# Depthwise convolution on TensorE: products in row order, copied out in token order

## The chip, the cores and the metric

One core of one Trainium2 chip. The metric is the device time of one execution in microseconds (us), median of three runs. Engines are named as the profile names them: PE is TensorE's matmul side and PEld its weight loads, DVE is VectorE, ACT is ScalarE, POOL is GpSimd, SP is SyncE.

## The reference, cut to what matters

The input is x, 4 images of 64 x 64 pixels with 256 channels, float32. Two layers follow each other. Layer 0, per pixel and per 2 x 2 window:

```
x_norm = layernorm(x);  x_proj, z = split(x_norm @ in_proj_W)          # 384 + 384 channels
y_ssm  = 0.5 * (scan over the 4 tokens of each 2x2 window, forward and backward)
y_dw   = depthwise 3x3 convolution of x_proj, padding SAME              # 9 taps, one weight per channel
y_conv = gelu(y_dw @ pw_W)
y      = (alpha * y_ssm + (1 - alpha) * y_conv) * silu(z) @ out_W
x_out  = x + y;  x = x_out + gelu(layernorm(x_out) @ fuse_W1 + b1) @ fuse_W2 + b2
```

Layer 1 is attention over the 4096 pixels of each image and a residual sum. The change touches only y_dw of layer 0.

## The kernel before, in words

Layer 0 walks over 32 tiles of 512 pixels (`TOK`), a tile being 8 rows of 64 pixels (`ROWS`). Within a tile the pixels are held in token order: the four positions (dr, dc) of a 2 x 2 window are four blocks of 128 pixels, inside a block by window row `wr` (4) and window column `wc` (32). Only `xp` (L217) is held in row order, with a border of one pixel: 10 rows of 66 floats for each of 3 channel blocks (`cb`). `inx` (L566, L569) fills it, and the convolution, the skip term (L595) and POOL's product (L689) read it.

The order of work is written out by hand in 48 ticks per tile: `OWN` lists the steps of tile k, `NEXT` the front steps of tile k+1, and `BACK` the closing steps of tile k-1. `body` (L529) gives PE, in each tick, three transposes of decay factors first (`turn_decays`, L510, one "fill" of a bank of `psD`), then the steps of the tick. DVE does the scan from these fills (`states`, L812: operations p, s, y), and its part of the other steps one tick later. The three `psD` banks let PE be three fills ahead: a fill waits for the DVE operation p (L865 or L868) that read the same bank three fills ago (L517 to L523).

The convolution of one channel block is three steps, a, b and c (rows dy = 0, 1, 2 of taps): ticks 8, 10, 11 for cb 0, ticks 13, 15, 17 for cb 1, ticks 19, 20, 21 for cb 2. A tap is a product with a diagonal matrix, `conv_w[:, cb, 3 * dy + dx, :]` (128 x 128, the tap's weights on the diagonal), accumulated over the nine taps in one bank of `psF`. Each tap has two products of 256 columns (L416 to L423), one for each row parity dr; its source takes every second row and, for each dc, every second pixel of `xp` (a step of two floats), so that the sums lie in PSUM in token order. After step c ACT copies the bank to `conv_sb` (the same memory as `y_ch`) in one instruction of 512 elements (L580). The pointwise product `pw` (L430, ticks 27 to 30) reads it.

`psF` has three banks, used in turn by the front jobs (`front_bank`, L121); PE waits for `front_out`, the count of ACT's copies, before it reuses one (L381). ACT's jobs are in the same order as PE's. Around the convolution stand the steps `ut` (PE transposes at L442, ACT copies at L608), `out` (PE at L470, after DVE's `y_ch` at L802), and in ticks 21 to 24 `xnt0`, `xnt1`, `xnth` (ACT L554, L557, DVE L758), `h2t` (ACT L622) and `w10` (PE L481, after L622). In tick 26 `proj` (PE L407) waits for DVE's L758.

The lines of PE's and ACT's part that the diff touches, with what calls them:

Of the kernel before, what the change touches and what calls it, by code (L numbers as in the profile page):

```python
# [14 lines left out]
ACT = mybir.ActivationFunctionType  # L15
# [5 lines left out]
B, H, W, C = 4, 64, 64, 256  # L21
# [10 lines left out]
ROWS = TOK // W  # L32
# [62 lines left out]
def exact(k):  # L95
    return isinstance(k, int)
# [67 lines left out]
def layer0(nc, keep, x, w, f_d, g_d, v_d, xres_d):  # L164
# [3 lines left out]
    with ctx:  # L168
# [18 lines left out]
        conv_w = sb("conv_w", [P, CB, 9, P])  # L187
# [29 lines left out]
        xp = sb("xp", [P, CB, ROWS + 2, W + 2])  # L217
# [19 lines left out]
        conv_sb = y_ch  # L237
# [129 lines left out]
        def _(pe):  # L367
# [3 lines left out]
            def front(step, f, par):  # L371
                if step.startswith(NOT_PSUM):
                    return
                kind, i = (step, "") if step in ("proj", "bct", "xnth") else (step[:-1], step[-1])
                job = step
                if step.startswith("conv"):
                    kind, i = "conv", step[4]
                    job = "conv" + i
                bank = psF[front_bank(f, job)]
                n, user = bank_user_before(f, job)  # L380
                if n is not None and not (kind == "conv" and step[-1] != "a"):  # L381
                    pe.wait_ge(front_out, n)
                    if user.startswith("xnt"):
                        pe.wait_ge(split_ok, SPLIT_JOBS * (iteration_of(f, job) + 2))
                if kind == "xnt":
                    if i == "0":
                        pe.wait_ge(stats1_ok, 5 * f + 5)
                    for t in range(T):
                        mm = turn(bank[:, t * P:(t + 1) * P], xf[:, t, int(i) * P:int(i) * P + P])
                elif kind == "xnth":  # L390
                    for kb in range(KB):
                        mm = turn(bank[:, kb * P:(kb + 1) * P], xf[:, T, kb * P:(kb + 1) * P])
                elif kind in ("inx", "z", "proj"):
                    if kind == "inx":
                        cb, dr = int(i) // 2, int(i) % 2
                        outs, src = bank[:, 0:TOK // 2 + W], [x[:, :, dr, :] for x in xnt]
                        wts = [x[:, :, cb * P:(cb + 1) * P] for x in in_w]
                    else:
                        outs = bank[:, :].rearrange("p (h n) -> p h n", h=2)
                        src = [x[:, :, :, 0:TOK // 2] for x in xnt]  # L400
                        c0 = INNER + int(i or 0) * P
                        wts = xproj_w if kind == "proj" else [x[:, :, c0:c0 + P] for x in in_w]
                    if kind == "proj":
                        pe.wait_ge(split_ok, SPLIT_JOBS * (f + 1))
                    for n, (a, b) in enumerate(((0, 0), (0, 1), (1, 0))):
                        for kb in range(KB):
                            mm = pe.matmul(outs, wts[a][:, kb, :], src[b][:, kb],  # L407
                                           start=n == 0 and kb == 0, stop=n == 2 and kb == KB - 1)
                elif kind == "bct":
                    pe.wait_ge(front_out, front_job(f, "proj"))  # L410
                    for t in range(T):
                        mm = turn(bank[:, t * P:(t + 1) * P], proj_sb[:, t * P:(t + 1) * P])
                elif kind == "conv":
                    cb, dy = int(i), "abc".index(step[-1])
                    for dx in range(3):
                        for dr in range(2):  # L416
                            src = xp[:, cb, dy + dr:dy + dr + ROWS - 1:2, dx:dx + W].rearrange(
                                "p wr (wc dc) -> p dc wr wc", dc=2)
                            mm = pe.matmul(bank[:, dr * 256:(dr + 1) * 256].rearrange(  # L419
                                "p (dc wr wc) -> p dc wr wc", dc=2, wr=ROWS // 2),  # L420
                                conv_w[:, cb, 3 * dy + dx, :], src,
                                start=dy == 0 and dx == 0, stop=dy == 2 and dx == 2,
                                skip_group_check=True)  # L423
                    if dy < 2:
                        return
                elif kind == "pw":
                    if i == "0":
                        pe.wait_ge(front_out, front_job(f, "conv2"))
                    for cb in range(CB):
                        mm = pe.matmul(bank[:, :], pw_w[:, cb, int(i) * P:int(i) * P + P], conv_sb[:, cb, :],  # L430
                                       start=cb == 0, stop=cb == CB - 1)
                elif step.startswith("dt"):
                    d, cb = "fb".index(step[2]), int(step[3])
                    r0 = 64 * d
                    mm = pe.matmul(bank[:, :], dt_w[r0:r0 + RANK, cb * P:(cb + 1) * P],
                                   proj_sb[r0:r0 + RANK, :], start=True, stop=True)
                elif step.startswith("ut"):
                    d, t = "fb".index(step[2]), int(step[3])
                    if t == 0:
                        pe.wait_ge(u_mul, 6 * f + 3 * (d + 1))  # L440
                    for cb in range(CB):
                        mm = turn(bank[:, cb * P:(cb + 1) * P], ut[:, cb, t * P:(t + 1) * P])  # L442
                mm.then_inc(front_full, 1)
# [98 lines left out]
        def _(act):  # L542
            def front(step, f, par):
# [28 lines left out]
                elif job == "proj":  # L572
                    last = nc.scalar.activation(proj_sb[:, :], bank[:, :], ACT.Identity, bias=proj_bias[:, :])
                elif job == "bct":
                    if not (exact(f) and f < 2):
                        act.wait_ge(state_ok, TILE_OPS * (f - 1))
                    src = bank[:, :].rearrange("p (t d r) -> p t d r", t=T, d=2)[:, :, :, RANK:RANK + 2 * STATES]
                    last = nc.scalar.activation(bc[:, par, :, :, :], src, ACT.Copy)
                elif job.startswith("conv"):
                    last = nc.scalar.activation(conv_sb[:, int(job[-1]), :], bank[:, :], ACT.Copy)  # L580
                elif job.startswith("dt"):
                    d, cb = "fb".index(job[2]), int(job[3])
                    if not (exact(f) and f == 0):
                        act.wait_ge(u_mul, 6 * (f - 1) + 3 * (d + 1))
                    last = nc.scalar.activation(dt[:, d, cb, :], bank[:, :], ACT.Silu,  # L585
                                                bias=col[:, dtb_c[d][cb]:dtb_c[d][cb] + 1])
                elif job.startswith("z"):
                    cb = int(job[-1])
                    if not (exact(f) and f == 0):
                        act.wait_ge(back_dve, emptied(f - 1, f"yt{cb}")[1])  # L590
                    for dr in range(2):
                        src = xp[:, cb, 1 + dr:dr + ROWS:2, 1:W + 1].rearrange("p wr (wc dc) -> p dc wr wc", dc=2)
                        dst = r_sb[:, cb, dr * 256:(dr + 1) * 256].rearrange(
                            "p (dc wr wc) -> p dc wr wc", dc=2, wr=ROWS // 2)
                        skip = nc.scalar.activation(dst, src, ACT.Copy, scale=mix[:, 2, cb:cb + 1])  # L595
                    skip.then_inc(skip_ok, 1)
                    last = nc.scalar.activation(q_sb[:, cb, :], bank[:, :], ACT.Silu,
                                                bias=in_bias[:, CB + cb:CB + cb + 1])
                elif job.startswith("pw"):
                    cb = int(job[-1])  # L600
                    if not (exact(f) and f == 0 and cb < 2):
                        act.wait_ge(r_ok, CB * f + cb - 1)
                    last = nc.scalar.activation(gel[:, cb % 2, :], bank[:, :], ACT.Gelu)
                elif job.startswith("ut"):
                    d, t = "fb".index(job[2]), int(job[3])
                    if t == 0 and not (exact(f) and f == 0):
                        act.wait_ge(state_ok, TILE_OPS * (f - 1) + DIR_OPS * (d + 1))
                    last = nc.scalar.activation(u[:, d, t, :], bank[:, 0:INNER], ACT.Copy)  # L608
# [845 lines left out]
```

## Time and profile before

| | |
|---|---|
| median of three runs | 5837.58 us |
| lowest and highest run | 5837.41 and 5845.89 us |
| span of the profiled execution | 5842.9 us, 100627 instructions |
| convolution products (L419) | 3456 records on PE, 397 ns each as listed |
| convolution copies (L580) | 96 on ACT |
| layer 0 | about the first 3560 us of the span |

No time of its own is given for the profiled execution; its span, first to last instruction, is 5.3 us (0.09%) over the median of the runs. A matmul with float32 operands shows as two records of PE and two weight loads: the 54 products of a tile (3 blocks x 9 taps x 2 parities) are 108 records, 12 in each of the nine steps. A record's listed length holds the time that it takes to pass through the array, so records overlap; what one costs PE is the distance from its start to the start of the next. A timeline merges like instructions that follow each other, with their number behind the x.

### The profile page before, as it was taken

How to read it: one execution, taken by the hardware profiler on the slowest of the kernel's cores; microseconds unless marked ns; L12 is line 12 of the kernel's file. 1: busy time of each engine (PE TensorE's matmuls, PEld its weight loads, DVE VectorE, ACT ScalarE, POOL GpSimd, SP SyncE). 2: the span in 40 equal slices, each digit the busy share in tenths (PEclk: the TensorE clock that was granted, in tenths of full speed). 3: DMA queues.
4: the chain of work that ended last, by engine and by line, in shares of the span. 5: the costliest groups of instructions: out<-in, count | busy, mean ns of one | idle time of the engine just before them, and what ended most of it. 6: DMA issues, size and time to landing. Idle time of an engine off the chain costs nothing. (4 is left out here: it accounts for less than half of the span.)

```text
span 5842.9 us, 100627 instructions
## 1 busy us (share of the span) xinstructions
PE 5433.9 (93%) x30696; PEld 4376.2 (75%) x30696; DVE 4398.7 (75%) x8598; ACT 3394.4 (58%) x5910; POOL 584.8 (10%) x658
## 2 busy tenths in 40 slices
PE   5999999999999999999999998899999999999998
PEld 4666666667667666666666665699889989988998
DVE  4888888887888788788878886676666667766666
ACT  3666666666666666666666664355555555555554
POOL 0111111111111110111111110100000000000000
PEclk8999999999999999999999999899999999999999
DMA  1010010010010010010000000300300030012000
GB/s 41 13 36 28 26 37 25 28 37 23 30 37 23 27 40 23 27 34 30 27 29 34 27 24 33 108 19 19 96 29 19 19 98 19 24 46 73 19 19 18
DMA packets 140892, 198.71 MB, mean 34 GB/s; under 512 B 19760, under 2 KB 107920, under 8 KB 140272
## 3 DMA queue, kind: packets, MB, share of 16 engines
q1 hardware_dynamic: 140272, 190.95, 10.3%
q8 instruction: 327, 5.36, 0.4%
q14 instruction: 293, 2.40, 0.1%
HBM read 111.22 MB, written 79.69 MB: 33 GB/s over the span
## 5 line engine op out<-in xcount | busy, mean ns | idle before, releaser
L1335 ACT ACTIVATE probs<-ps_s 128x512 f32<-128x512 f32 x1024 | 612.3, 598 | 1037.6 <-PE ps_s L1288 1037.6
L1346 DVE TENSOR_REDUCE part_max<-ps_m 128x1 f32<-128x512 f32 x1056 | 717.2, 691 | 576.1 <-PE ps_m L1268 575.9
L1297 PE MATMUL ps_o<-vh,ph 128*128 128x258 f32 x4096 | 1045.7, 288 | 31.6 <-ACT ph L1337 31.6
L1298 PE MATMUL ps_o<-vl,ph 128*128 128x256 f32 x4096 | 1037.1, 285 | 0.0
L369 PEld LDWEIGHTS psD<-ident,dec 128*128 128x128 f32 x4608 | 572.5, 144 | 491.0 <-DVE p_st L868 142.3
L369 PE MATMUL psD<-ident,dec 128*128 128x128 f32 x4608 | 784.2, 284 | 160.0 <-ACT dec L653 79.3
L868 DVE TENSOR_TENSOR p_st<-s_st,psD 128x384 f32<-128x384 f32 x1024 | 561.8, 549 | 490.0 <-PE psD L369 486.0
L419 PE MATMUL psF<-xp,conv_w 128*128 128x256 f32 x3456 | 862.4, 398 | 10.7 <-ACT u L608 10.3
L1297 PEld LDWEIGHTS ps_o<-vh,ph 128*128 128x128 f32 x4096 | 789.4, 193 | 48.1 <-issue 23.5
L653 ACT ACTIVATE dec<-dt,decay 128x384 f32<-128x384 f32 x1536 | 804.6, 603 | 2.3
L1298 PEld LDWEIGHTS ps_o<-vl,ph 128*128 128x128 f32 x4096 | 789.5, 193 | 0.0
L1370 DVE TENSOR_TENSOR pl<-probs,ph 128x512 fp32r<-128x512 f32 x1024 | 711.4, 695 | 69.6 <-ACT ph L1337 55.3
L419 PEld LDWEIGHTS psF<-xp,conv_w 128*128 128x128 f32 x3456 | 631.7, 189 | 155.8 <-ACT u L608 18.0
L1303 PEld LDWEIGHTS ps_o<-vh,pl 128*128 128x128 f32 x4096 | 627.9, 192 | 107.9 <-DVE pl L1370 34.7
L1303 PE MATMUL ps_o<-vh,pl 128*128 128x258 f32 x4096 | 681.3, 289 | 0.3
L871 DVE SCALAR_TENSOR_TENSOR s_st<-u,bc,p_st 128x384 f32<-128x384 f32 x1024 | 659.0, 651 | 0.0
L881 DVE SCALAR_TENSOR_TENSOR y_tok<-s_st,bc,y_tok 128x384 f32<-128x384 f32 x960 | 618.9, 645 | 0.0
L1337 ACT ACTIVATE ph<-ps_s 128x512 fp32r<-128x512 f32 x1024 | 608.5, 594 | 0.0
L689 POOL TENSOR_TENSOR ut<-dt,xp 128x256 f32<-128x256 f32 x384 | 341.6, 923 | 1886.8 <-ACT dt L585 1886.7
L1268 PE MATMUL ps_m<-f_max,gq 96*128 96x512 f32 x1056 | 416.7, 418 | 32.8 <-DMA gq<-queries_d 29.9
L1288 PE MATMUL ps_s<-gq,f_st 128*128 128x512 f32 x1024 | 409.6, 405 | 39.2 <-issue 37.4
L865 DVE SCALAR_TENSOR_TENSOR p_st<-u,bc,psD 128x384 f32<-128x384 f32 x512 | 303.2, 607 | 171.9 <-PE psD L369 100.9
(145 smaller groups left out, 7055.8 us busy)
## 6 DMA issues: line engine op xcount, KB each, us to landing
values_d<-v_st SPq DMA_DIRECT2D x64, 512.0 KB, 4.8
xf<-in_x_dram SPq DMA_DIRECT2D x128, 128.0 KB
xb<-in_x_dram SPq DMA_DIRECT2D x128, 128.0 KB
residual_d<-xb SPq DMA_DIRECT2D x32, 512.0 KB, 2.6
vh<-values_d SPq DMA_DIRECT2D x32, 512.0 KB, 5.0
vl<-values_d SPq DMA_DIRECT2D x32, 512.0 KB, 6.0
res<-residual_d SPq DMA_DIRECT2D x32, 512.0 KB, 3.3
out_dram<-res SPq DMA_DIRECT2D x128, 128.0 KB
```

The source lines that it names most:

```text
L369: return pe.transpose(out, in_, ident[:, :])
L419: mm = pe.matmul(bank[:, dr * 256:(dr + 1) * 256].rearrange("p (dc wr wc) -> p dc wr wc", dc=2, wr=ROWS // 2), conv_w[:, cb, 3 * dy + dx, ...
L653: nc.scalar.activation(dec[:, pair8 % 2, n, cb, :, :], dt[:, d, cb, first * P:(first + 3) * P].rearrange("p (t w) -> p t w", t=3), ACT.Exp ...
L871: nc.vector.scalar_tensor_tensor(s_t, u[:, d, token_of(d, step), :], scalar(step, n, "b"), p_t, ALU.mult, ALU.add).then_inc(state_ok, 1)
L881: nc.vector.scalar_tensor_tensor(y_t, src, scalar(step, n, "c"), y_t, ALU.mult, ALU.add).then_inc(state_ok, 1)
L1297: pe.matmul(ps_o[qt][:, 0:C + 2], lhs, vh[:, m, :], start=m == 0, stop=False, skip_group_check=True)
L1298: pe.matmul(ps_o[qt][:, 0:C], lhs, vl[:, m, :], start=False, stop=False, skip_group_check=True)
L1303: mm = pe.matmul(ps_o[qt][:, 0:C + 2], pl[:, m % 3, qt * P:(qt + 1) * P], vh[:, m, :], start=False, stop=m == KEYS - 1, skip_group_check=True)
L1335: nc.scalar.activation(probs[:, m % 3, :], ps_s[m % 2][:, :], ACT.Exp).then_inc(exp_ok, 1)
L1337: nc.scalar.activation(ph[:, m % 3, :], ps_s[m % 2][:, :], ACT.Exp).then_inc(exp_ok, 1)
L1346: nc.vector.tensor_reduce(part_max[:, qt, kc:kc + 1], ps_m[r % 2][:, :], AX.X, ALU.max).then_inc(max_out, 1)
L1370: nc.vector.tensor_tensor(pl[:, m % 3, :], probs[:, m % 3, :], ph[:, m % 3, :].bitcast(F32), ALU.subtract).then_inc(pl_ok, 1)
```

## The change

Each tap becomes one product of 512 columns whose source is 8 rows of 64 pixels of `xp`, in row order, and whose output is the whole bank in row order. ACT's copy becomes two ACTIVATEs of 256 elements, one for each dr, which read the bank with a step of two floats and write `conv_sb` in token order. The waits, the semaphore counts and the tick table stay.

```diff
                     for dx in range(3):
-                        for dr in range(2):
-                            src = xp[:, cb, dy + dr:dy + dr + ROWS - 1:2, dx:dx + W].rearrange(
-                                "p wr (wc dc) -> p dc wr wc", dc=2)
-                            mm = pe.matmul(bank[:, dr * 256:(dr + 1) * 256].rearrange(
-                                "p (dc wr wc) -> p dc wr wc", dc=2, wr=ROWS // 2),
-                                conv_w[:, cb, 3 * dy + dx, :], src,
-                                start=dy == 0 and dx == 0, stop=dy == 2 and dx == 2,
-                                skip_group_check=True)
+                        mm = pe.matmul(bank[:, :].rearrange("p (r w) -> p r w", r=ROWS), conv_w[:, cb, 3 * dy + dx, :],
+                                       xp[:, cb, dy:dy + ROWS, dx:dx + W],
+                                       start=dy == 0 and dx == 0, stop=dy == 2 and dx == 2)
...
                 elif job.startswith("conv"):
-                    last = nc.scalar.activation(conv_sb[:, int(job[-1]), :], bank[:, :], ACT.Copy)
+                    for dr in range(2):
+                        src = bank[:, :].rearrange("p (wr dr wc dc) -> p dr dc wr wc", dr=2, dc=2, wr=ROWS // 2)
+                        last = nc.scalar.activation(
+                            conv_sb[:, int(job[-1]), dr * 256:(dr + 1) * 256].rearrange(
+                                "p (dc wr wc) -> p dc wr wc", dc=2, wr=ROWS // 2), src[:, dr], ACT.Copy)
```

## Rows read from the trace of the kernel before

**Rows 1.** The page: busy time, share of the span, instructions; clock in 40 slices.

```profile
PE 5433.9 (93%) x30696; PEld 4376.2 (75%) x30696; DVE 4398.7 (75%) x8598; ACT 3394.4 (58%) x5910; POOL 584.8 (10%) x658
...
PEclk8999999999999999999999999899999999999999
```

**Rows 2.** Windows: length; PE, PEld, DVE, ACT, POOL busy (xcount); granted clock; DMA share; GB/s.

```profile
0.00:3560.00 3560.00, 3288.08 (x15771) 2404.66 (x15772) 2844.24 (x5891) 2229.41 (x3794) 460.52 (x520) 0.96 0.09 29
1649.10:1681.00 31.90, 31.57 (x166) 26.18 (x166) 25.61 (x68) 16.39 (x31) 3.75 (x4) 1.00 0.00 1
1681.00:1725.00 44.00, 41.36 (x196) 28.15 (x194) 33.59 (x63) 30.33 (x52) 5.51 (x6) 1.00 0.08 28
1612.00:1616.00 4.00, 3.58 (x14) 2.05 (x13) 4.00 (x8) 4.00 (x10) 0.40 (x1) 0.66 0.02 4
1625.00:1637.00 12.00, 10.77 (x33) 5.96 (x32) 7.85 (x16) 7.66 (x11) 4.78 (x6) 0.58 0.37 134
```

**Rows 3.** Source line L419: lengths in ns min/median/max, first and last start.

```profile
L419 PEld LDWEIGHTS psF<-xp,conv_w x3456: 185/188/193, 110.2 to 3558.9; 128*128 128x128 f32 x192
L419 PE MATMUL psF<-xp,conv_w x3456: 387/397/497, 110.2 to 3559.1; 128*128 128x256 f32 x192
```

**Rows 4.** Timeline of PE: start us, us, line, tiles, shape, xcount [idle before <-releaser].

```profile
1641.96 2.97 PE L419 MATMUL psF<-xp,conv_w 128*128 128x256 f32 x12
...
1645.90 2.86 PE L470 MATMUL psB<-out_w,y_ch 128*128 128x256 f32 x12 [0.64 <-DVE y_ch L802]
...
1651.74 2.75 PE L470 MATMUL psB<-out_w,y_ch 128*128 128x256 f32 x12
1654.33 0.49 PE L369 MATMUL psD<-ident,dec 128*128 128x128 f32 x3
...
1658.96 3.09 PE L419 MATMUL psF<-xp,conv_w 128*128 128x256 f32 x12 [0.34 <-ACT u L608]
...
1662.54 0.49 PE L369 MATMUL psD<-ident,dec 128*128 128x128 f32 x3
...
1676.76 2.98 PE L419 MATMUL psF<-xp,conv_w 128*128 128x256 f32 x12
1679.59 0.60 PE L369 MATMUL psF<-ident,xf 128*128 128x128 f32 x4
...
1682.84 1.96 PE L481 MATMUL psB<-xt,w 128*128 128x512 f32 x4
...
1687.38 1.64 PE L407 MATMUL psF<-xnt,xproj_w 128*128 128x512 f32 x6 [0.21 <-DVE xnt L758]
...
1690.90 2.74 PE L430 MATMUL psF<-y_ch,pw_w 128*128 128x512 f32 x6
1693.48 0.49 PE L369 MATMUL psD<-ident,dec 128*128 128x128 f32 x3
```

**Rows 5.** Groups of ACT by shape, 1000 to 1800 us: xcount | busy us, mean ns.

```profile
L595 ACT ACTIVATE r_sb<-xp,mix 128x256 f32<-128x256 f32 x42 | 20.3, 532 | 37.3 <-DVE y_ch L802 37.3
...
L580 ACT ACTIVATE y_ch<-psF 128x512 f32<-128x512 f32 x23 | 13.7, 597 | 97.7 <-PE psF L419 97.7
...
L557 ACT ACTIVATE xnt<-psF 128x256 fp32r<-128x256 f32 x8 | 3.1, 387 | 0.0
```

**Rows 6.** Timeline of DVE, columns as in rows 4.

```profile
1654.86 0.55 DVE L868 TENSOR_TENSOR p_st<-s_st,psD 128x384 f32<-128x384 f32 x1 [3.52 <-PE psD L369]
...
1659.41 0.60 DVE L865 SCALAR_TENSOR_TENSOR p_st<-u,bc,psD 128x384 f32<-128x384 f32 x1
...
1680.99 0.55 DVE L868 TENSOR_TENSOR p_st<-s_st,psD 128x384 f32<-128x384 f32 x1 [2.41 <-PE psD L369]
```

**Rows 7.** Timeline of ACT, columns as in rows 4.

```profile
1658.42 0.49 ACT L608 ACTIVATE u<-psF 128x384 f32<-128x384 f32 x1
...
1679.78 0.60 ACT L580 ACTIVATE y_ch<-psF 128x512 f32<-128x512 f32 x1 [4.49 <-PE psF L419]
...
1681.91 0.78 ACT L622 ACTIVATE xt<-psB,col 128x512 f32<-128x512 f32 x1
```

## The prediction

> **What bounds the kernel now.** The page comes first: PE is busy 93% of the span, DVE 75%, ACT 58% [rows 1]. Those are averages over two layers, so the windows come next. Layer 0 is the first 3560 us; PE works in 3288 of them at a mean granted clock of 0.96 of full, DVE in 2844 [rows 2]. The convolution of one tile runs from 1641.96 to 1679.59 [rows 4]. From 1649.1 to 1681, PE is busy 31.57 of 31.90 us at clock 1.00 and DVE 25.61 of 31.90 [rows 2]. PE's only idle time there is one wait of 0.34 us for ACT's `u` copy [rows 4]. DVE, on its side, sits idle twice for a fill of `psD`, 3.52 and 2.41 us [rows 6]. So in this stretch PE sets the pace and DVE waits for it. Behind it, from 1681 to 1725, PE is busy 41.36 of 44.00 us [rows 2], so time saved in the convolution isn't waited for again there. Only ahead of it does DVE lead: PE stands idle for 0.64 us before `out0` (L470), for DVE's `y_ch` [rows 4].
>
> **What a product costs now.** A tile's convolution is nine steps of 12 records of 256 columns. One step, from its start to the next instruction's, is 1679.59 - 1676.76 = 2.83 us, some 235 ns a record [rows 4]. Two neighbours tell what the same work costs elsewhere. `out1` (L470) is also 12 float32 records of 256 columns, with a source whose floats lie side by side: 1654.33 - 1651.74 = 2.59 us, 216 ns a record. `pw0` (L430) is six float32 records of 512 columns, again from such a source: 1693.48 - 1690.90 = 2.58 us, 430 ns a record [rows 4]. Two things follow. First, 512 columns at once cost what 2 x 256 cost (430 against 2 x 216), so halving the number of products and weight loads is worth nearly nothing by itself; a weight load of 188 ns [rows 3] fits behind a record of 216 to 235 already. Second, the convolution pays 19 ns a record more than `out1`, and the difference that I see between the two is the source with its step of two floats and its runs of 32.
>
> **The change, part by part.** (1) PE. A step becomes six records of 512 columns from rows of 64 neighbouring floats. Bounds for one step: 2.58 us, as `pw0`, and 2.82 us (12 x 235 ns), if all of the surcharge stays. The merged lengths say the same, 2.74 against 2.98. I take 2.58, since `pw0` is the same shape, type and count and the new source has its floats side by side; what is left unlike is the gap between rows. Gain 0.24 us a step. The Trainium skill, SBUF — State Buffer, section "Door 1: The DMA port swizzle", in its note on cachelines, says that SBUF is read in lines of 16 bytes, that at least two hits on a line are needed for full speed, and that every new line costs something. By that rule two of four floats a line should just be absorbed and the gain be doubtful; the 19 ns show that it is not absorbed, so the trace decides.
>
> (2) How many of the nine steps count. `conv0a` (1641.96) lies ahead of the wait of 0.64 us for `y_ch`; DVE's time there doesn't move, so its 0.24 only makes that wait 0.88. The other eight count: 8 x 0.24 = 1.92 us a tile.
>
> (3) What is late next. Between DVE's two waits lie seven of the eight steps, 7 x 0.24 = 1.7 us. DVE's second wait of 2.41 us shrinks to some 0.7, so DVE doesn't yet become the bound. PE would run earlier against DVE in between, and could meet a bank of `psD` not yet read. The closest place is the fill at 1662.54 [rows 4], whose bank DVE read in the p at 1659.41 for 0.60 us [rows 6]: 2.53 us of room, against 0.5 us saved by then. No new wait.
>
> (4) ACT's copy. One instruction of 597 ns becomes two of 256 elements. Lower bound: two like L557, 387 ns, overlapping by 0.10 us as L580 and the instruction after it do in the timeline (next start 1680.28): 0.68 us, or 0.08 more. Upper bound: two like L595, which moves 256 elements with the same step of two floats, 532 ns each [rows 5]: 0.97, or 0.37 more. A step of two floats out of PSUM is not in the trace. I take 0.15 more, near the lower end, because L557 reads PSUM too and L595 reads SBUF and has a scale operand besides. ACT is idle 4.49 us before the third copy [rows 7] and its total is of no account, so only what is queued behind a copy counts. After `conv0c` that is `u` (L608), on which PE waits 0.34 us, but it starts only at 1658.42 [rows 7], 0.14 us after the copy has ended (1657.68 + 0.60), as PE's transposes are late: nothing. After `conv2c`, the copy at 1679.78 leads straight into the two `xnt` and two `xt` copies, the last of which ends at 1681.91 + 0.78 = 1682.69 [rows 7]; `w10` starts at 1682.84 [rows 4]. So 0.15 us reaches PE. It might be taken up again at `proj`, which waits 0.21 us for DVE at 1687.38 [rows 4]. I charge it in full. The `pw` products that read the copies come at 1690.90, 11 us later: nothing. No DMA, semaphore or queue is touched, and POOL reads `xp`, not the bank.
>
> (5) The sum. 1.92 - 0.15 = 1.77 us a tile. The first tile has no closing steps of an earlier one and DVE leads after its convolution, so I count 31: 55 us. Against the profiled execution 5842.9 - 55 = 5788 us; that span is 5.3 us over the median of the runs, so against the median 5837.6 - 55 = **5783 us**. Layer 1 has none of these instructions.
>
> **The rivals.** *The surcharge belongs to the row starts.* Each record of now has 8 runs (4 window rows, 2 dc), each new one has 8 rows. If the 19 ns are the price of 8 starts, a step costs 6 x (430 + 19) = 2.69 us, gains 0.13, and the kernel 31 x (8 x 0.13 - 0.15) = 28 us: 5810. For it: nothing in the trace has gaps without a step. Against it: little either.
>
> *A record costs by its columns alone.* The surcharge would then be something that this operand keeps whatever its order, 2 x 235 ns a record. PE gains nothing, the copy's 0.15 us remain: 31 x 0.15 = 5 us slower, 5842, no change that can be told. Against it stands `out1` at 216. The Trainium skill, TensorE: Matmul & The Clock Gate, section "Back-to-back issue gap", has this rule: a gap of columns over the clock plus 2.5 ns. By it six records fewer a step would save 15 ns, some 4 us in all, and the result would be no change as well.
>
> *The clock.* PE's granted clock is 0.66 in the 4 us from 1612, after PE had waited for ACT, and 0.58 in the 12 us from 1625 [rows 2]: stretches at 1.2 GHz between those at 2.4. If PE's new pauses bring one more like the first in each tile, where PE leads, it costs 4 x 0.34 = 1.4 us a tile, 42 in all: 5825. If they take that one away, the kernel gains as much again: about 5741.
>
> *The slower end: ACT's read of PSUM with a step.* Place: the copies after `conv0c` and `conv2c`, where PE waits on ACT. An element costs (597 - 387) / 256 = 0.82 ns [rows 5]. At twice that a copy takes 0.42 + 0.08 = 0.5 us more, 1.0 a tile with both waits, and 28 us of gain remain. It decides from 0.96 us more per copy (two waits against 1.92). At four times the element's price it is 1.35, and the kernel loses 31 x (2.70 - 1.92) = 24 us: 5862. Nothing in the trace reads PSUM so; L595 reads SBUF so and is only 0.15 over L557.
>
> **How the numbers follow.** About 0.2% (12 us) is what a measurement of this kernel can tell from no change. Forecast (5770 to 5797) 0.60; row starts, 5810, 0.13; columns alone, 5842, 0.09; the clock against, 5825, 0.06, half of it within 12 us; the clock in favour, 0.07; the copy, 5862, 0.05. Faster by over 0.2%: 0.60 + 0.13 + 0.03 + 0.07 = 0.83. Within: 0.09 + 0.03 = 0.12. Slower: 0.05. The range runs from 5755, which takes in `conv0a` (7 us) and some time at the lower clock won back, to 5827, past the row starts and the clock against; it leaves out the two last cases and the far end of the good clock, some 0.2.
>
> **What would show it.** L419 with 1728 records of 512 columns, 430 ns from start to start, a step of 2.58 us (2.69: row starts; 2.82: columns alone). L580 as 192 instructions, a pair in some 0.75 us. The wait before `out0` at 0.88, DVE's waits near 3.3 and 0.7, `w10` 0.15 later after its copy. Tiles 1.8 us shorter each, layer 1 as long as before. The forecast is wrong if the steps measure 2.58 and the tile is not shorter: then the time sits in a new wait of PE on DVE behind the convolution, or in the clock.

## The result, and the profile after

The changed kernel takes 5733.56 us (median of four runs, 5727.62 to 5743.48) against 5837.49 us before (four runs, 5831.98 to 5845.89): ratio 0.9817, 95% interval 0.9802 to 0.9832. That is 104 us, nearly twice the 55 that were forecast, and below the range.

First the page of the changed kernel: busy time per engine, and the granted clock in 40 slices.

```profile
PE 5328.4 (93%) x28968; PEld 4033.1 (70%) x28968; DVE 4389.0 (77%) x8598; ACT 3396.8 (59%) x6006; POOL 590.7 (10%) x658
...
PEclk7999999999999999999999998899999999999999
```

PE has 1728 records fewer and 105 us less busy time, almost exactly what the kernel gained [rows 1]; the share stays at 93%. Next, all instructions of the convolution (in the changed kernel L416 is the product, L577 the copy), from the view of a source line; columns as in rows 3.

```profile
L416 PEld LDWEIGHTS psF<-xp,conv_w x1728: 186/189/192, 110.2 to 3462.7; 128*128 128x128 f32 x192
L416 PE MATMUL psF<-xp,conv_w x1728: 590/592/697, 110.2 to 3463.1; 128*128 128x512 f32 x192
```

```profile
L577 ACT ACTIVATE y_ch<-psF x192: 377/382/387, 119.2 to 3464.1; 128x256 f32<-128x256 f32 x192
```

A record of 512 columns is listed with 592 ns, as `pw0` was before (593). From the first to the last start of the convolution it is 96 us less than in rows 3. The timeline of PE in one tile answers to rows 4.

```profile
1604.46 2.74 PE L416 MATMUL psF<-xp,conv_w 128*128 128x512 f32 x6
1608.62 2.86 PE L465 MATMUL psB<-out_w,y_ch 128*128 128x256 f32 x12 [1.09 <-DVE y_ch L801]
...
1621.19 2.84 PE L416 MATMUL psF<-xp,conv_w 128*128 128x512 f32 x6 [0.34 <-ACT u L607]
...
1637.79 2.74 PE L416 MATMUL psF<-xp,conv_w 128*128 128x512 f32 x6
1640.37 0.60 PE L369 MATMUL psF<-ident,xf 128*128 128x128 f32 x4
...
1643.68 1.96 PE L476 MATMUL psB<-xt,w 128*128 128x512 f32 x4 [0.21 <-ACT xt L621]
...
1648.16 1.64 PE L407 MATMUL psF<-xnt,xproj_w 128*128 128x512 f32 x6
```

A step is 1640.37 - 1637.79 = 2.58 us, as forecast. The wait before `out0` has grown to 1.09 (forecast 0.88), the wait for `u` stands at 0.34, `w10` now shows 0.21 us of waiting, and `proj`'s wait of 0.21 [rows 4] is gone. Counted from the end of the last step, `w10` starts after 3.31 us and before after 3.25, but `proj` after 7.79 us in both kernels: the small delay behind the copy is taken up there. DVE's two waits for a fill, to be set against rows 6, and ACT's last copy with what follows, against rows 7:

```profile
1617.34 0.56 DVE L867 TENSOR_TENSOR p_st<-s_st,psD 128x384 f32<-128x384 f32 x1 [3.28 <-PE psD L369]
1641.77 0.55 DVE L867 TENSOR_TENSOR p_st<-s_st,psD 128x384 f32<-128x384 f32 x1 [1.24 <-PE psD L369]
```

```profile
1640.57 0.66 ACT L577 ACTIVATE y_ch<-psF 128x256 f32<-128x256 f32 x2 [3.77 <-PE psF L416]
1641.11 0.60 ACT L549 ACTIVATE xnt<-psF 128x512 fp32r<-128x512 f32 x1
```

The pair of copies takes 0.66 us, against 0.60 for the one of before.

So the convolution does what was forecast. Where is the other half? In a stretch without any changed instruction: the end of each tile, from PE's pause in tick 42, in which it waits 2.29 us for ACT's `dec`, to the first fill of the next tile. Here are windows from the end of that pause to the first fill of the next tile, for tiles 12 and 13 (counted from 0) of the kernel before, and below the same for the kernel after. Columns as in rows 2; the last but two is the granted clock.

```profile
1502.60:1514.00 11.40, 10.70 (x51) 7.42 (x52) 9.69 (x18) 8.81 (x19) 0.91 (x1) 0.85 0.11 28
1611.50:1624.00 12.50, 11.02 (x50) 7.43 (x50) 10.62 (x20) 9.26 (x19) 0.90 (x1) 0.86 0.12 30
```

```profile
1470.20:1480.10 9.90, 9.22 (x50) 6.68 (x51) 9.18 (x17) 8.46 (x19) 0.89 (x1) 1.00 0.06 14
1576.20:1587.10 10.90, 9.39 (x50) 6.62 (x50) 10.19 (x19) 9.01 (x19) 0.96 (x1) 1.00 0.08 20
```

The same work takes 11.40 and 12.50 us before, 9.90 and 10.90 after, and the granted clock is 0.85 against 1.00: a part of the stretch ran at 1.2 GHz before and all of it at 2.4 after. I read 29 tile ends (tiles 1 to 29) of every run in this way. Before, the clock falls in 28 of them, after in 8. In each of these tile ends the low stretch begins close to the end of the pause, between 0.3 us before it and 2.3 us after it, in the kernels before and after and in the experiments without the pause filled (e1 to e4, e7, e8). The pause itself is 2.29 us in both kernels, first before, then after:

```profile
1611.76 0.54 PE L369 MATMUL psD<-ident,dec 128*128 128x128 f32 x3 [2.29 <-ACT dec L653]
```

```profile
1576.52 0.54 PE L369 MATMUL psD<-ident,dec 128*128 128x128 f32 x3 [2.29 <-ACT dec L652]
```

A ledger of tiles 1 to 30 puts the gain in its places. Each tile is cut at four places of PE's trace: the start of `conv0a`, the end of `conv2c`, the start of the last instruction ahead of the pause of tick 42, and the start of the first `dt` product (L435) of the next tile. Sums over 30 tiles in us; the other kernels are explained below.

| | convolution | behind it | pause and tile end | head of the next tile | all |
|---|---|---|---|---|---|
| before | 1136.5 | 1266.6 | 443.8 | 471.7 | 3318.6 |
| after | 1076.2 | 1266.5 | 403.0 | 477.7 | 3223.5 |
| e4 | 1136.7 | 1266.7 | 442.1 | 474.0 | 3319.5 |
| e5 | 1127.9 | 1266.7 | 393.7 | 483.5 | 3271.7 |
| e7 | 1157.2 | 1266.6 | 427.5 | 471.9 | 3323.2 |
| e8 | 1093.8 | 1266.6 | 428.2 | 479.3 | 3267.9 |
| e10 | 1127.0 | 1266.6 | 392.2 | 488.0 | 3273.7 |
| e11 | 1088.0 | 1266.5 | 435.3 | 478.8 | 3268.6 |
| e12 | 1072.1 | 1266.6 | 391.8 | 485.9 | 3216.4 |

From before to after, the convolution gives 60 us, the tile ends give 41, and the heads take 6 back.

### The profile page after: what moved, and what is told of

Its sections match the earlier page's. It is cut to its first block and busy times, and to the rows that moved or that the text cites. A ratio compares the mean times of both kernels' runs of the same rounds, so it can differ in the third digit from the quotient of the medians.

```text
span 5733.2 us, 97267 instructions
## 1 busy us (share of the span) xinstructions
PE 5328.4 (93%) x28968; PEld 4033.1 (70%) x28968; DVE 4389.0 (77%) x8598; ACT 3396.8 (59%) x6006; POOL 590.7 (10%) x658
## 5 line engine op out<-in xcount | busy, mean ns | idle before, releaser
L867 DVE TENSOR_TENSOR p_st<-s_st,psD 128x384 f32<-128x384 f32 x1024 | 562.0, 549 | 393.8 <-PE psD L369 393.7
L416 PE MATMUL psF<-xp,conv_w 128*128 128x512 f32 x1728 | 792.8, 594 | 10.7 <-ACT u L607 10.3
L416 PEld LDWEIGHTS psF<-xp,conv_w 128*128 128x128 f32 x1728 | 306.8, 189 | 298.3 <-issue 276.8
```

The costliest lines, as they stand in the source:

```text
L416: mm = pe.matmul(bank[:, :].rearrange("p (r w) -> p r w", r=ROWS), conv_w[:, cb, 3 * dy + dx, :], xp[:, cb, dy:dy + ROWS, dx:dx + W], star ...
```

## The experiments

Two questions. Is the source's step of two floats the surcharge of the product? And why does the clock no longer fall at the tile's end: because tiles are shorter and the pause falls elsewhere (theory one), or because the convolution now has fewer products and weight loads (theory two)? The ratios are to the kernel before, timed beside each group on the same chip: 5846.25 us beside e1 to e4, 5841.19 beside e5 to e8, 5844.30 beside e9 to e12. Kernels of different groups are therefore best compared by their ratios; the changed kernel's is 0.9817. All kernels but e5 and e7 start from the changed kernel.

**e1, e2: count and step apart.** e1 keeps two products, in row order; e2 makes one product that takes every second float.

```diff
e1
+for h in range(2):
+    pe.matmul(bank[:, h * 256:(h + 1) * 256] (rows of 64), conv_w[...], xp[:, cb, dy + 4 * h:dy + 4 * h + 4, dx:dx + W], ...)
e2
+    xp[:, cb, dy:dy + ROWS, dx:dx + W].rearrange("p r (wc dc) -> p dc r wc", dc=2)
```

> Each tap as two products of 256 columns again, but in row order (rows 0 to 3, rows 4 to 7), source floats side by side, copy as in the changed kernel. If the source's step of two floats was the surcharge: 3456 records, 216 ns from start to start, a step of 2.59 us, time as the changed kernel, 5735 us within 12. If the number of products was what counted: 235 ns a record, 2.82 us a step, 5790 to 5840 us.

> Each tap as one product of 512 columns, but its source takes every second float (all even pixels of the 8 rows, then all odd ones); the copy's order is adapted. If the step of two floats is the surcharge: 1728 records, 470 ns from start to start, a step of 2.82 us, and the time goes back to 5790 (its 60 us alone) or to 5837 (if the granted clock falls in every tile again as it did before). If the number of products was what counted: 430 ns a record, 5735 us.

The groups by shape, 1000 to 1800 us, first of e1, then of e2 (xcount | busy us, mean ns):

```profile
L417 PE MATMUL psF<-xp,conv_w 128*128 128x256 f32 x756 | 174.4, 379 | 2.3 <-ACT u L610 2.3
```

```profile
L416 PE MATMUL psF<-xp,conv_w 128*128 128x512 f32 x403 | 198.9, 627 | 2.3 <-ACT u L608 2.3
```

In e1 a record of 256 columns is 379 ns long, 19 less than the 398 of before at the same length; from start to start it is 216, and a step is 2.59 us. In e2 a record of 512 is 627 long instead of 594, and a step is 2.79. So the step of two floats is the surcharge, and the number of products and weight loads is worth 0.01 to 0.03 us a step (2.59 against 2.58, 2.82 against 2.79). One thing changes with the step in e2: a record then has 16 runs of 32 floats and not 8 of 64. The 8 runs of the changed kernel cost nothing that shows (430 ns, as `pw0`), so starts of runs are an unlikely cause, but no run here has short runs without the step. The times were 5764.24 us (ratio 0.9854, 0.9838 to 0.9871) and 5815.85 us (0.9947, 0.9930 to 0.9964). e1 has the changed kernel's cheap steps and is still 29 us over the expected 5735: its clock falls at 18 of 29 tile ends, e2's at 23. This was the first sign that the clock doesn't belong to one form of the product. It also shows how loosely the count of low ends hangs on PE's work: the changed kernel, e3 and e1 have the same work in the convolution to 0.01 us a step, and 8, 13 and 18 low ends. Each count comes from one trace.

**e3: the copy.** ACT's one plain copy; the permutation is left out.

> The changed kernel with ACT's one plain copy of 512 elements as before; it leaves the permutation into token order out, so the convolution's pixels stand in row order. If the second ACTIVATE costs what I charged (0.15 us a tile at w10): 5 us less than the changed kernel, about 5729. If it costs nothing on the path: 5734. If the copy was dear (0.5 us in two places): 5705.

Measured 5738.15 us, ratio 0.9811 (0.9795 to 0.9827), with the clock low at 13 of 29 ends. It can't be told from the changed kernel: the difference looked for is 5 us, and each low end is worth 1.5 to 1.6. e9 repeats it below.

**e4: the old amount of work in the new form.** One more product per step, weights of zero, 144 columns.

```diff
 for dx in range(3):
+    if dx == 2:
+        pe.matmul(bank[:, 0:144], zero_w[:, :], conv_w[:, 0, 0:2, :] (144 columns), start=False, stop=False, ...)
```

> The changed kernel with one more product in each of the nine steps, 144 columns with weights of zero (2 records, some 0.24 us), which adds nothing to the sums: PE's work per tile is that of the kernel before, in another form. Theory one (half of the gain is the clock: it depends on when PE's wait for ACT's dec falls, and so on the tile's length): the granted clock falls again once near the end of every tile, two tiles take 221.8 us as before, 5837 within 15. Theory two (the clock follows the weight loads or the form of the products): two tiles take 215 + 2 x 1.95 = 218.8 us with as few low stretches as the changed kernel, 5795 us.

Measured 5837.73 us over ten runs, ratio 0.9982 (0.9973 to 0.9992). A step is 2.82 us as before, two tiles take 221.7 us, and all 29 tile ends are low. Two of them, tiles 12 and 13:

```profile
1502.10:1513.70 11.60, 10.87 (x51) 7.44 (x52) 9.71 (x18) 8.83 (x19) 0.94 (x1) 0.85 0.11 28
1611.20:1624.40 13.20, 11.04 (x51) 7.27 (x51) 11.30 (x21) 9.31 (x19) 0.95 (x1) 0.87 0.11 28
```

Theory two expected 5795. With eight records a step, six of 512 columns and two of 144, in the place of twelve of 256, and the old length of the tile, the ledger of e4 is that of the kernel before within 2.3 us in each place, the clock is low again, and the 0.2% by which e4 is faster is about the 9 us that its layer 1 is shorter in the traces. 60 us of work put back took back 96: by the ratios 0.9982 - 0.9817, and in the ledger 3319.5 - 3223.5.

**e5, e6: the pause filled.** PE gets two products of constants while it waits for `dec` in tick 42; the fill that follows overwrites them. For this the wait for the bank moves ahead of the wait for `dec`. e5 is the kernel before with this, e6 the changed kernel.

```diff
-pe.wait_ge(dec_ok, ...)
 ... (wait for the bank, state_ok)
+if pair8 == 2 * PAIRS - 1 and j == 0:
+    for _ in range(2):
+        pe.matmul(psD[0][:, :], ident[:, :], conv_w[:, 0, 0:4, :] (512 columns), start=True, stop=True)
+pe.wait_ge(dec_ok, ...)
```

> The kernel before with two products of 512 columns (ident times conv_w, overwritten by the fill that follows) put into the pause of 2.3 us in which PE waits for ACT's dec in tick 42. They take 1.72 us and end inside the pause. If the pause is what brings the low clock at each tile's end, it stays away and 1.6 us a tile are won: 5837 - 50 = 5787 us. If the low stretch has another cause (the clock falls there whatever PE does in the pause): 5837, no change.

> The changed kernel with the same two products in the same pause. Its trace has a low stretch at a tile's end in 8 of 31 tiles: if the pause brings them, up to 8 x 1.6 = 13 us less, 5720 us. If not: 5734. If the products run past the pause: a few us more than 5734.

PE's timeline in e5, around the pause, and then the ends of its tiles 12 and 13:

```profile
1595.24 1.88 PE L525 MATMUL psD<-conv_w,ident 128*128 128x512 f32 x4
1597.61 0.55 PE L369 MATMUL psD<-ident,dec 128*128 128x128 f32 x3 [0.49 <-ACT dec L657]
```

```profile
1489.30:1499.30 10.00, 9.28 (x51) 6.74 (x52) 9.29 (x17) 8.62 (x19) 1.01 (x1) 1.00 0.06 15
1597.30:1608.80 11.50, 9.45 (x51) 6.67 (x51) 10.79 (x20) 9.06 (x19) 1.03 (x2) 1.00 0.10 25
```

The idle time before the fill is 0.49 instead of 2.29 us, the clock is 1.00 at all 29 ends in both kernels, and e5 takes 5788.3 us (ratio 0.9907, 0.9891 to 0.9924), as expected: 53 us faster than the kernel before by doing more. In the traces 42 of them lie in layer 0; the rest comes from layer 1, which the edit doesn't touch (see the account below). e6 takes 5736.09 us (0.9814, 0.9798 to 0.983), no different from the changed kernel as a whole, of whose low ends only 8 were left; its layer 0 is 6 us shorter.

**e7, e8: a third of the work.** The zero-weight product in the three steps with dy = 1, in the kernel before (e7) and in the changed one (e8).

> The kernel before with one more product of 144 columns and weights of zero (2 records, 0.24 us) in three of the nine steps (dy = 1), so 0.7 us more PE work a tile. Theory one (the clock depends on the tile's length): not linear; two tiles take either 221.8 + 1.5 = 223.3 with the low stretch in every tile (5860 us), or less than 221.8 if the stretches stay away in part: anything from 5800. Theory two (linear, clock as before): 5837 + 31 x 0.73 = 5860 us.

> The changed kernel with the same product in three of the nine steps, 0.7 us more PE work a tile, about a third of what the change took away. Linear: 5734 + 31 x 0.73 = 5757 us. Theory one (the low clock comes back as the tile's length nears the old one): more than that, 5757 to 5790, by 1.6 us for each tile whose clock falls at its end.

e8: 5793.83 us, ratio 0.9909 (0.9891 to 0.9927), 22 of 29 ends low. By the ratios that is 54 us for 23 us of work, but not all of it is the clock. In the traces layer 1 has 13 us of it, and in layer 0 PE stands still 13 times, once every second tile, for 15 us in all, with nothing that it waits for in the profile; e11 shows this more clearly below. e7: 5836.52 us over ten runs, ratio 0.9989 (0.998 to 0.9999), 27 of 29 low: 23 us of work cost nothing that can be told. That fits neither expectation. In the profiled executions its layer 0 was 10 us longer than before's and its layer 1 15 us shorter. The ledger has the work, 21 us more in the convolution, and 16 us less at the tile ends: there the low stretch begins 0.4 us after the end of the pause on average, against 1.5 in the kernel before, and costs less.

**e9 to e12: the same with the pause filled.** e12 is e6 once more; e9 has the plain copy, e10 the extra product in nine steps, e11 in three.

> The changed kernel with the pause filled, again, as the partner of the run with the plain copy: 5736 us, ratio 0.981, no low stretch at a tile's end.

> The changed kernel with the pause filled, and with ACT's one plain copy (the permutation is left out): the price of the second ACTIVATE with the clock out of play. As charged (0.15 us a tile): 5 us under the same kernel with both ACTIVATEs. Not on the path: the same within 3 us.

> The changed kernel with both additions: the zero-weight product of 144 columns in all nine steps, and the two products in PE's pause of tick 42 that keep it at work there. With the clock held at the tile's end, the time should follow PE's work in a line: 5736 (only the pause filled) + 31 x 8 x 0.245 = 5797 us, ratio 0.992 or a little less, no low stretch at a tile's end. If the pause doesn't matter in this kernel: 5838 as without it, ratio 0.998.

> The same with the zero-weight product in three of the nine steps. On the line with the clock held: 5736 + 31 x 0.73 = 5759 us, ratio 0.985 to 0.986. Without the pause filled this work made 5794 (ratio 0.991); if the filling does nothing here, that is what comes again.

| | us | ratio (95%) | low ends of 29 |
|---|---|---|---|
| e12 | 5744.55 | 0.9824 (0.9810 to 0.9838) | 0 |
| e9 | 5741.57 | 0.9821 (0.9807 to 0.9835) | 0 |
| e10 | 5798.28 | 0.9919 (0.9903 to 0.9935) | 0 |
| e11 | 5782.44 | 0.9893 (0.9877 to 0.9909) | 0 |

e12 and e9 are the same within their intervals, but those are 8 us to either side, so the times alone can't exclude the 5 us. The traces are closer: layer 0 ends at 3570.2 us in e9 and at 3570.2 and 3570.8 in e6 and e12. The second ACTIVATE costs nothing on the path that shows. e10 is as expected: the 60 us of work now cost 54 (5798.28 - 5744.55; 59 in layer 0) and not 96.

e11 is a miss: 38 us for 23 us of work, with no low end in these windows. The ledger has 16 us of the work in the convolution and 43.5 us more in the column of the tile end, and most of that is not the clock: once after each of the 13 jumps of the loop, whose body is two tiles, PE stands still for 2.4 to 3.1 us in the middle of a fill, 38 us in all. One of them:

```profile
1603.67 0.43 PE L370 MATMUL psD<-ident,dec 128*128 128x128 f32 x2 [0.96 <-DVE s_st L879]
1606.96 0.33 PE L370 MATMUL psD<-ident,dec 128*128 128x128 f32 x1 [2.86 <-issue]
```

The profile names nothing that PE waits for there ("issue"). In this one the clock still stands at 1.00 from 1603.7 to 1607 and falls after it, so the clock is not its cause. Only e11 and, with 15 us in all, e8 have this standstill; the other twelve traces have no such idle time over 0.8 us in the tiles of the loop. These two kernels have the same convolution, and why it comes in them was not tested. Windows over two such heads of e11, then one of e12:

```profile
1603.70:1619.00 15.30, 12.44 (x37) 7.25 (x38) 10.82 (x20) 7.38 (x11) 5.07 (x6) 0.67 0.36 120
1821.90:1837.00 15.10, 11.95 (x33) 6.32 (x34) 8.83 (x18) 5.96 (x8) 4.85 (x6) 0.55 0.36 122
```

```profile
1583.00:1598.00 15.00, 11.41 (x55) 7.01 (x56) 12.97 (x25) 9.66 (x14) 4.81 (x6) 1.00 0.37 126
```

## Why the prediction was wrong

**The account.** Layer 0 ends where layer 1's first product starts. That was 3671.9 us before, 3630.2 in e5 (pause filled), 3570.2 in e6 and 3576.5 in the changed kernel. With the clock held at the tile's end by the filled pause in both, the change takes 3630.2 - 3570.2 = 60 us off layer 0; e10 against e12 gives 59. Filling the pause takes 3671.9 - 3630.2 = 42 us off the old kernel, the net price of its low clock at the tile's end, and 3576.5 - 3570.2 = 6 off the new one. Together 60 + 35 = 95 us of layer 0, and the ledger, which needs no experiment, says the same (60 + 41 - 6). The profiled executions differ by 14 us more in layer 1, where no instruction has changed:

```profile
3671.90:5842.90 2171.00, 2071.85 (x14632) 1922.45 (x14632) 1498.97 (x2599) 1129.09 (x2063) 113.96 (x128) 0.97 0.14 40
```

```profile
3576.50:5733.20 2156.70, 2066.84 (x14632) 1916.77 (x14632) 1499.89 (x2599) 1129.59 (x2063) 114.48 (x128) 0.97 0.14 41
```

The first is before, the second after. It isn't a matter of the instructions, which are the same: e6 and e12, the same kernel, have 2166.3 and 2173.6 us there, and over all the profiled executions it lies between 2154.8 and 2173.6. It goes with the clock: 150 us of layer 1 ran at 1.2 GHz before and 133 after, and in the shortest and longest layer 1 of the fourteen traces it is 127 and 156 us. What decides that is open, and what it adds to the difference of the medians, I can't say closer than these 19 us.

**Right, by its own steps.** The bound: PE paces the convolution and keeps what it is given. The product: 2.58 us a step, and the surcharge is the source's step of two floats (e1, e2), not its row starts (2.69) and not something tied to the columns (2.82). The rule of the Trainium skill, SBUF — State Buffer, section "Door 1: The DMA port swizzle", that two hits on a line give full speed, does not hold for this operand of PE: e2's records are 627 ns long against 594. The same note's penalty for each new line points the way that was measured; no run parts it from the step. The count of eight steps: 31 x 8 x 0.24 = 60 us, measured 59 to 60. DVE did not become the bound. The time between its two waits is 1.7 us shorter, as forecast, but its second wait is 1.24 us where I had written 0.7, since 0.21 us came off a small wait between them and some 0.3 I can't place; and no wait for a bank of `psD` appeared in the convolution.

**Off in size.** Step (4), ACT's copy, was charged 0.15 us a tile. The pair takes 0.06 us more than the single copy, at the lower bound: reading PSUM with a step of two floats has no price in this trace (382 ns for 256 elements, L557 387). `w10` starts 0.06 us later, and `proj`'s old wait for DVE takes it up. The price on the path is none that a run could show, so 5 of the 55 us were taken off for nothing.

**The step that failed.** Step (5), the sum, has no term for the clock: it adds PE's 1.92 us and ACT's 0.15 and leaves the low clock in each tile as it was. What the runs showed in its place is a term of some 35 us: the low stretch at the tile's end, worth a net 42 us in the old kernel, mostly went away (28 of 29 ends before, 8 after; 41 us less at the tile ends in the ledger). The rival "the clock" had this term with about the right price, 1.4 us a tile, measured (3671.9 - 3630.2) / 31 = 1.35; but it gave the favourable side a chance of 0.07 and no reason for so little, and the range left it out. It also tied the low stretch to new pauses of PE that would take it away. The pause ahead of it did not change, 2.29 us in both kernels, and the low stretch went away all the same.

e5 and e6 show that the pause is needed: with it filled, no end is low. e4 shows that with the old amount of PE work per tile the low stretch is back at every end, whatever the form of the products. The pause and the length of the tile (or the PE work in it; the runs don't part the two) decide together, and not strictly, as 8, 13 and 18 low ends with the same work show. Why a shorter tile loses fewer stretches is open. The trace of before had a warning in it: the low stretch came at the same place in 28 of 29 tiles. Something as regular as that may be tied to the tile's length, and the change shortened the tile. That the rival's number, 5741, was only 7 us off is in part luck: the copy's 5 us that it took off were not there, and layer 1 gave up to 14 us that nobody had counted.

## What to carry to other kernels

A float32 product whose moving operand takes every second float of SBUF costs PE 9% more than one that takes neighbours (235 against 216 ns per 256 columns); read rows as they lie and let the copy out of PSUM permute, which cost 0.06 us in 0.60 here. Where a low clock stands at the same place in every pass of a loop, price it as a term of its own in both directions before changing the length of the pass: here 60 us of work moved layer 0 by 95 us or by 60, depending on whether the clock came along. And before a surprise is put down to the clock, look for idle time on PE that waits for nothing: in e11 it was 38 us. A pause of PE can be filled with products that are overwritten; that gave the old kernel 53 us and the new one nothing that its time shows, so it isn't a version that beats the changed kernel.

## What the hardware showed that I had not expected

More work made a kernel faster (e5, 53 us). And 23 us of work, put in without the pause filled, cost nothing in one kernel (e7) and some 54 us in another (e8), of which 15 are a standstill of PE after the loop's jump and 13 lie in layer 1.

The times of two tiles, from the start of the convolution in tile 4 to that in tile 28 divided by twelve, lie close together for different amounts of work: 221.8 (before), 221.7 (e4), 221.9 (e7); 218.4 (e8), 218.6 (e5), 218.6 (e10), 218.7 (e11); 215.2 (after), 214.8 (e6), 214.7 (e9, e12). They don't only take these values: e1, e2 and e3 lie between them with 216.5, 220.3 and 216.0. And one of the meetings is a coincidence of sums: e10 has six extra products more than e11, 1.5 us of PE work a tile, and e11 stands still for 2.9 us every two tiles. Whether there is more behind the rest, I did not test. What decides when the low clock comes at the tile's head stays open, as does layer 1's spread of 19 us.
